# A depthwise convolution moved from per-lag steps to one triangular product per channel, in a fused conditional residual block

## The reference, cut to what matters

```python
x = x + depthwise_causal_conv(x, w=cond)            # x: (B=32, T=32, C=256) f32, cond: (K=32, C=256)
ada = cond @ ada_w + ada_b                          # six chunks: shift, scale, gate, twice
h = ln(x) * (1 + scale1) + shift1                   # layer norm over C, one (shift, scale) per batch
q, k, v = split(h @ qkv_w + qkv_b)                  # 16 heads of 128
a = softmax(q k^T / sqrt(128)) v                    # within a batch: 32 x 32 scores
y = x + gate1 * (a @ out_w + out_b)
g = gelu((ln(y) * (1 + scale2) + shift2) @ ffn_w1 + ffn_b1)
out = x + y + gate2 * (g @ ffn_w2 + ffn_b2)
```

## Time and profile before

| | |
|---|---|
| median of 3 runs | 336.91 us (336.74 to 336.94) |
| profiled execution, first to last instruction | 337.2 us |
| PE busy | 319.7 us, 95% |
| PE weight loads | 269.0 us, 80% |
| DVE busy | 180.0 us, 53% |
| ACT, POOL busy | 152.7 us, 80.8 us |

### The profile page before, as it was taken

The page is one execution under the profiler, slowest core; times in us unless marked ns, Lnnn a source line. Parts: engine busy times, 40 slices in busy tenths (PEclk is TensorE's granted clock), DMA queues, the critical chain, the costliest instruction groups (busy, mean ns, idle before and its releaser), DMA issues.

```text
span 337.2 us, 6425 instructions
## 1 busy us (share of the span) xinstructions
PE 319.7 (95%) x2655; PEld 269.0 (80%) x2655; DVE 180.0 (53%) x354; ACT 152.7 (45%) x269; POOL 80.8 (24%) x78
## 2 busy tenths in 40 slices
PE   5969599999999999999999999999999999899994
PEld 4959496868888888888888888888898778588884
DVE  4959979866606224333441532631625699783232
ACT  6421032423366525526625535653443557742910
POOL 5606510031034103006303003500201444430400
PEclk9959789999999999999999999999999999999998
DMA  7822100010004202002300101210200000000011
GB/s 247 318 68 62 62 3 0 2 65 0 0 2 126 64 0 64 0 2 68 122 0 0 62 0 41 86 63 0 64 2 0 3 2 0 0 2 0 0 64 62
DMA packets 9607, 14.56 MB, mean 43 GB/s; under 512 B 520, under 2 KB 5744, under 8 KB 9584
## 3 DMA queue, kind: packets, MB, share of 16 engines
q1 hardware_dynamic: 9536, 14.19, 12.9%
q10 hardware_dynamic: 48, 0.03, 0.0%
HBM read 13.18 MB, written 1.05 MB: 42 GB/s over the span
## 4 chain that ended last, share of the span: by engine, by line
PE 79%; DVE 17%; issue 1%; DMA 1%; ACT 1%; DVEq 0%
PE bank L930 16%; PE bank L931 16%; PE bank L932 16%; PE bank L1006 7%; DVE xc L537 6%; PE bank L939 4%; PE bank L941 4%; PE bank L940 4%; PE bank L863 3%; PE bank L992 3%; PE bank L853 3%; DVE pt L642 2%; DVE yacc L747 1%; DVE xc L547 1%; DMA crow<-in_cond_dram 1%
## 5 line engine op out<-in xcount | busy, mean ns | idle before, releaser
L278 POOL TENSOR_TENSOR wl<-raw,wh 128x512 fp32r<-128x512 f32 x40 | 53.1, 1349 | 181.2 <-ACT wh L333 181.2
L930 PE MATMUL bank<-x1h,wl 128*128 128x512 f32 (+1 forms) x176 | 67.8, 385 | 0.0
L931 PE MATMUL bank<-x1l,wh 128*128 128x512 f32 (+1 forms) x176 | 65.9, 374 | 0.0
L932 PE MATMUL bank<-x1h,wh 128*128 128x512 f32 (+1 forms) x176 | 65.8, 374 | 0.0
L394 ACT ACTIVATE pool<-bank,bg 128x512 f32<-128x512 f32 x56 | 38.6, 688 | 57.3 <-PE bank L932 57.0
L653 DVE SCALAR_TENSOR_TENSOR ol<-bank,bT,oh 128x512 fp32r<-128x512 f32 x32 | 23.9, 749 | 46.8 <-ACT oh L423 46.0
L537 DVE SCALAR_TENSOR_TENSOR xc<-x,condT,xc 128x240 f32<-128x240 f32 (+32 forms) x114 | 39.4, 417 | 0.0
L930 PEld LDWEIGHTS bank<-x1h,wl 128*128 128x128 f32 x176 | 34.0, 193 | 6.3 <-issue 0.7
L931 PEld LDWEIGHTS bank<-x1l,wh 128*128 128x128 f32 x176 | 34.0, 193 | 5.8 <-issue 0.2
L932 PEld LDWEIGHTS bank<-x1h,wh 128*128 128x128 f32 x176 | 33.9, 193 | 5.7
L1006 PEld LDWEIGHTS bank<-pt,pool 128*128 128x128 f32 x256 | 31.9, 191 | 3.4 <-issue 0.9
(11 more groups left out here) (105 smaller groups left out, 450.8 us busy)
## 6 DMA issues: line engine op xcount, KB each, us to landing
raw<-in_L_cond_qkv_w_dram SPq DMA_DIRECT2D x12, 512.0 KB, 3.8
raw<-in_L_cond_out_w_dram SPq DMA_DIRECT2D x4, 512.0 KB, 3.4
raw<-in_L_cond_ffn_w_dram SPq DMA_DIRECT2D x4, 512.0 KB, 3.4
adaw<-in_L_cond_ada_w_dram SPq DMA_DIRECT2D x1, 1024.0 KB, 11.3
out_dram<-pool SPq DMA_DIRECT2D x4, 256.0 KB, 2.2
pool<-in_x_dram SPq DMA_DIRECT2D x2, 256.0 KB, 3.1
adaw<-in_L_cond_ada_w_dram SPq DMA_DIRECT2D x1, 512.0 KB, 5.3
pool<-in_x_dram SPq DMA_DIRECT2D x1, 512.0 KB, 6.1
```

Of the source, the lines that this page charges most:

```text
L278: g.tensor_tensor(wl[:, cols], raw[:, cols], wh[:, cols].bitcast(F32), ALU.subtract)\
L930: pe.matmul(dst, wl[:, w_cols], a_hi, start=start, stop=False)
L931: pe.matmul(dst, wh[:, w_cols], a_lo, start=False, stop=False)
L932: return pe.matmul(dst, wh[:, w_cols], a_hi, start=False, stop=stop)
```

## The change

The lags, the diagonals and `x0`'s part in the convolution go. In their place:

1. x is loaded in two pieces of 512 KB. It is spread from (batch in tile, time) x channel to `xq`, whose partitions are 4 channel groups of 64 x 32 time steps. That is 16 copies of 32 partitions x 512 elements, 5 on ACT and 11 on DVE. Source runs stride over 256 elements.
2. `cond` is written to a new DRAM tensor `cond_padded` with 31 rows of zeros behind it: two DMAs on ACT's queue, one DRAM to DRAM (32 rows), one from an SBUF tile of zeros (31 rows). SP waits for both, then reads `toep` back in four DMAs of 256 KB, each to 32 partitions, with overlapping source rows. `toep[:, j, :, c]` is then the 32x32 triangular matrix of channel slot c of group j, in 128 rows of which the others are zeros. The zeros are four memsets of 128x2048, two on DVE, two on POOL.
3. `conv(k)`, k = 0 to 3: 64 products each, stationary `toep[:, j, :, c]` (128x32, elements 256 bytes apart), moving `xq[:, c]` (128x32), into partition group j of bank `CB[k]`. 256 products do the whole convolution for all tokens.
4. Four copies of 128x512 take it to `conv_out` (ACT 0 and 2, DVE 1 and 3).
5. `turn(n)`, n = 0 to 3: 32 products each, stationary `conv_out[:, 32 slots, batch]` (elements 128 bytes apart), moving `pick` (128x64, zeros and ones), bring it to channels on partitions. They accumulate on x's transposes, which were put into the same banks `XB[n]` with no end of group, so that the residual sum needs no other instruction. Four copies take the banks to `xc`.
6. Order: all of this stands ahead of the norms. `modulation(1)` and `(2)` become one, ahead of `project_chunk(0)`. `mean(2)`, `var(2)`, `spread(2)` stand among the chunk projections, and the first attention joins the regular `unit(0, 1, first=True)`. The biases' DMAs move from SP's queue to ACT's; ada_w stands ahead of the first group's weights. POOL's clearing of `pt` waits for the turns, because `conv_out` lies in its memory.

```diff
-    PE_LAGS = [[0] + list(range(6, 17)), [0] + list(range(3, 18)), [0] + list(range(8, 15))]
-    DVE_LAGS = [[j for j in range(1, T) if j not in lags] for lags in PE_LAGS]
+        XB, CB = PB + YB[0:1], [S_BANK, OB[0], OB[1], YB[1]]
+        cond_pad = nc.dram_tensor("cond_padded", [QB, 2 * T - 1, SLOTS], F32)
+        def pad_rows(r0, r1):
+            return bass.AP(cond_pad, r0 * SLOTS, [[SLOTS, r1 - r0], [(2 * T - 1) * SLOTS, QB], [1, SLOTS]])
+        SPREAD_BY_ACT = [(i, g) for g in range(QB) for i in range(QB)][1::3]
...
@@ sync
-            load_x(0)
-            load_x(1)
+            for n in range(HALVES):
+                sp.dma_start(xtok[:, 4 * n:4 * n + 4, :], x_v[:, 4 * n:4 * n + 4, :]).then_inc(s_x[n], 16)
+            sp.wait_ge(s_pad, 32)
+            for g in (0, 2, 1, 3):
+                sp.wait_ge(s_tz[g // 2], g % 2 + 1)
+                sp.dma_start(toep[T * g:T * (g + 1), g, :, :].rearrange("p u s -> p (u s)"),
+                             bass.AP(cond_pad, g * (2 * T - 1) * SLOTS, [[SLOTS, T], [1, T * SLOTS]]))\
+                    .then_inc(s_toep, 16)
             load_adaw(0, 0, ADA1 * P)
-            load_x(2)
...
+            load_adaw(1, ADA1 * P, ADA * P)
             load_group(0)
-            load_adaw(1, ADA1 * P, ADA * P)
...
@@ gpsimd
-            for n in range(1, ND, 2):
...
+            for q in (2, 3):
+                g.memset(toep[:, q, :, :], 0.0).then_inc(s_tz[1], 1)
...
@@ scalar
             a.dma_start(crow[:, :], cond).then_inc(s_row[0], 16)
+            a.dma_start(pad_rows(0, T), cond.rearrange("k (g s) -> k g s", g=QB)).then_inc(s_pad, 16)
+            a.wait_ge(s_zr, 1)
+            a.dma_start(pad_rows(T, 2 * T - 1), zrows[:, :].rearrange("k (g s) -> k g s", g=QB)).then_inc(s_pad, 16)
+            for at, src in ((B_QKV, qkv_b), (B_ADA, ada_b), (B_OUT, out_b), (B_F1, ffn_b1), (B_F2, ffn_b2)):
...
+            for i, g in SPREAD_BY_ACT:
+                a.activation(xq[T * g:T * (g + 1), :, i, :],
+                             xtok[T * i:T * (i + 1), :, SLOTS * g:SLOTS * (g + 1)].rearrange("p n s -> p s n"),
+                             ACT.Copy).then_inc(s_xq[0], 1)
...
@@ vector
-            conv(0, 0, len(DVE_LAGS[0]))
-            conv_sum(0)
+            for g in range(QB):
+                for i in range(QB):
+                    if (i, g) not in SPREAD_BY_ACT:
+                        v.tensor_copy(xq[T * g:T * (g + 1), :, i, :],
+                                      xtok[T * i:T * (i + 1), :, SLOTS * g:SLOTS * (g + 1)]
+                                      .rearrange("p n s -> p s n")).then_inc(s_xq[1], 1)
+            conv_copy(1)
+            conv_copy(3)
+            xc_copy(1)
             centre(0)
...
@@ tensor
+            def conv(k):
+                if k == 2:
+                    pe.wait_ge(s_btc, 1)
+                if k == 3:
+                    pe.wait_ge(s_cond, 1)
+                for s in range(CBLK):
+                    c = CBLK * k + s
+                    for j in range(QB):
+                        m = pe.matmul(CB[k][T * j:T * (j + 1), B * s:B * (s + 1)], toep[:, j, :, c],
+                                      xq[:, c, :, :].rearrange("p i n -> p n i"), start=True, stop=True)
+                m.then_inc(s_cv, 1)
+            def turn(n):
+                if n == 0:
+                    pe.wait_ge(s_co[0], 2)
+                    pe.wait_ge(s_co[1], 2)
+                    pe.wait_ge(s_const, 4)
+                tiles = XB[n][:, :].rearrange("p (k b t) -> p k b t", k=CT, b=XB_B)
+                for b in range(XB_B):
+                    for q in range(QB):
+                        s0 = T * (q % 2)
+                        m = pe.matmul(tiles[T * q:T * (q + 1), :, b, :], conv_out[:, s0:s0 + T, XB_B * n + b],
+                                      pick[:, q // 2, :, :], start=False, stop=(b == XB_B - 1), skip_group_check=True)
+                m.then_inc(s_sel, 1)
+            pe.wait_ge(s_toep, 16 * QB)
+            pe.wait_ge(s_xq[0], len(SPREAD_BY_ACT))
+            pe.wait_ge(s_xq[1], QB * QB - len(SPREAD_BY_ACT))
+            for k in range(NX):
+                conv(k)
...
+            turn(0)
+            turn(1)
+            mean(0)
             pe.wait_ge(s_adaw[0], 16)
             modulation(0)
-            mean(0)
-            conv(1, 0, 2)
             var(0)
-            conv(1, 2, 4)
+            turn(2)
+            mean(1)
             spread(0)
-            conv(1, 4, len(PE_LAGS[1]))
+            turn(3)
+            var(1)
+            pe.wait_ge(s_adaw[1], 16)
+            pe.wait_ge(s_adat, ADA_STEPS[0])
+            modulation(1)
...
             pe.wait_ge(s_lo, CT)
             pe.wait_ge(s_adat, 2)
-            project_chunk(0, (0,))
-            mean(1)
...
-            conv(2, 0, 4)
+            project_chunk(0, (0, 1))
+            spread(1)
+            project_chunk(0, (2, 3))
+            mean(2)
+            project_chunk(0, (4, 5))
             pe.wait_ge(s_lo, CT * 2)
-            project_chunk(1, range(0, 5))
+            project_chunk(1, (0,))
+            var(2)
+            project_chunk(1, (1, 2))
+            spread(2)
+            project_chunk(1, (3, 4))
             scores(0, 0)
             project_chunk(1, (5,))
-            conv(2, 4, len(PE_LAGS[2]))
...
-            modulation(1)
...
-            project(0, 1, range(0, 9))
-            scores(0, 1)
-            project(0, 1, (9, 10, 11))
+            pe.wait_ge(s_lo, CT * 3)
+            pe.wait_ge(s_adat, ADA_STEPS[1])
+            unit(0, 1, first=True)
             with pe.Fori(1, NG - 1) as hg:
```

More of the change, by code:

```diff
@@ L84, in cond_resid_block_kernel @@
         pool = sb("pool", [P, 16 * PIECE])
+        with nc.sbuf_tensor("conv_out", [P, SLOTS, B], F32) as conv_out:
+            pass
         pt = sb("pt", [P, HALVES, GH, TG, P])
+        with nc.sbuf_tensor("adaw", [P, CT, ada_w.shape[1]], F32) as adaw:
+            pass
         oh = sb("oh", [P, GH, HT], F32R)
@@ L91, in cond_resid_block_kernel @@
         ident = sb("ident", [P, P])
+        pick = sb("pick", [P, 2, CT, T])
+        zrows = sb("zrows", [T - 1, C])
         ones = sb("ones", [P, P])
@@ L105, in cond_resid_block_kernel @@
         vt = sb("vt", [P, TG, T])
-        with nc.sbuf_tensor("diag", [P, ND, P], F32) as diag, \
-                nc.sbuf_tensor("adaw", [P, CT, ada_w.shape[1]], F32) as adaw:
+        with nc.sbuf_tensor("toep", [P, QB, T, SLOTS], F32) as toep:
             pass
@@ L513, in _ @@
         def _(v):
+            v.memset(zrows[:, :], 0.0).then_inc(s_zr, 1)
+            for q in (0, 1):
+                v.memset(toep[:, q, :, :], 0.0).then_inc(s_tz[0], 1)
             v.wait_ge(s_condt, 1)
-            v.tensor_copy(condT[:, :, :], S_BANK[:, 0:CT * B].rearrange("p (k b) -> p k b", k=CT))\
+            v.tensor_copy(condT[:, :, :], CB[3][:, 0:CT * B].rearrange("p (k b) -> p k b", k=CT))\
                 .then_inc(s_cond, 1)
-            v.wait_ge(s_xt, 1)
-            for ct in range(CT):
-                v.tensor_copy(part(x0, ct, CHUNKS[0]), OB[0][:, 256 * ct:256 * (ct + 1)]).then_inc(s_xe[0], 1)
@@ L713, in _ @@
             softmax_transpose(0, 0)
-            conv_sum(2)
-            centre(2)
-            o_low(0, 0, (0, 1))
-            scale_up(2)
-            var_eps(2)
-            o_low(0, 0, (2,))
-            norm(2)
-            shift(2)
-            o_low(0, 0, (3,))
-            x1_low(2)
-            modulation(1)
-            modulation(2)
-            add_y(0, 0, first=True)
-            one_plus(2, SCALE2)
-            softmax_front(0, 1)
-            softmax_back(0, 1)
+            unit(0, 1, first_y=True)
             unit(1, 0, first_y=True)
@@ L842, in conv @@
-            def conv(n, i0, i1):
-                nt, last = CHUNKS[n][1], len(PE_LAGS[n]) - 1
-                for i in range(i0, i1):
-                    j = PE_LAGS[n][i]
-                    for ct in range(CT):
-                        d = DIAG_LAGS.index(j)
-                        pe.wait_ge(s_diag[ct], d + 1)
-                        xs = by_batch(part(x0, ct, CHUNKS[n]))
-                        dst = by_batch(CONV_BANKS[n][ct][:, 0:nt])
-                        m = pe.matmul(dst[:, :, j:], diag[:, CT * d + ct, :], xs[:, :, :T - j],
-                                      start=(i == 0), stop=(i == last))
-                        if i == last:
-                            m.then_inc(s_cpe, 1)
@@ L858, in mean @@
-            def mean(n):
-                pe.wait_ge(s_const, 2)
-                pe.wait_ge(s_in, CT * (n + 1))
+            for n in range(NX):
+                pe.wait_ge(s_x[n // 2], 16)
+                for i in range(2 * CT):
+                    ct, t = divmod(i, 2)
+                    pe.matmul(XB[n][:, P * i:P * (i + 1)], xtok[:, 2 * n + t, ct * P:(ct + 1) * P], ident[:, :],
+                              start=(i == 0), stop=False, is_transpose=True, skip_group_check=True)
+            pe.wait_ge(s_row[1], 16 * 5)
```

255 lines of the change are left out of this document (110 added, 145 removed).

## The result

The changed kernel takes 334.14 us (median of 20 executions, 332.06 to 337.12), the kernel before 337.99 us beside it (20 executions, 336.74 to 339.52). The ratio is 0.9887, with a 95% interval of 0.986 to 0.9914 (it leaves out the one of the 20 executions that is more than 1.5% above its kernel's fastest, 337.12 us). So the change makes the kernel 1.1% faster, 3.9 us where 19.2 were forecast.

A forecast was written before the change was run, and what follows sets the result against it. PE's instruction list was taken as the bound, except where DVE's lags held it. First projection 3.2 us later, at 37.5, and units 19.2 us earlier gave a span of 318.0, median 317.7 us; range 312.3 to 325.5.

The forecast's parts named there:

- the convolution starts: Start of PE's convolution products: expected at 13.7 us, once x has landed and been spread.
- the convolution: PE's 256 small products: 7.7 us, at the scores' pace with the first 5 us at half clock.
- the handover: Between convolution and turns: the last `conv_copy`, 0.69 us, and a handover of 0.15 us.
- from the turns to the first projection: PE's list of turns, means, variances, modulations and spread before the first projection: 15.3 us without a wait.
- the regular units and the end: Everything from the first regular unit onward: no instruction's work altered, only reached 19.2 us earlier.
- rival 2: Convolution and turns: strided operands halve the small products' pace, +5.2 us each, total 328 us; chance 0.12.
- the clock that I had put at half for 5 us: Convolution: after about 7 us idle, PE runs 123 products at half clock for 5 us.
- Rival 4: Convolution and turns: four partition groups stop overlapping, 41 ns per product, +31 us, total 349 us; chance 0.05.
- rival 1: Convolution start: zero rows' write lands at about 13, convolution 4.2 us late, 322 us; or clock wakes late, 323; chance 0.20.
- My cover of 3.6 us for `toep`: Before the convolution: `toep` loads landed by 10 us, hidden behind x's spreading with 3.6 us to spare.
- Stretch two: First projection to the regular units: 72.4 us before, 22.4 us leave it, becoming 50.0 us.
- From span to time: Whole kernel: the median time was taken to lie 0.3 us below the span, 318.0 to 317.7 us.

The follow-up runs named there:

- e1: Changed kernel with the convolution's stationary operand reading neighbouring elements of toep (output not the reference's): 331.1 us, one execution.
- e3: Changed kernel with both operands of the convolution read in the order of memory (output not the reference's): 332.67 us, ratio 0.9816.
- e9: Changed kernel with the convolution as a loop of 8 passes over 32 products, strides kept (output not the reference's): 334.9 us, one execution.
- e8: Changed kernel with the convolution as a loop of 8 passes over 32 products, operands neighbouring (output not the reference's): 328.0 us, one execution.
- e7: Changed kernel with both convolution operands in memory order, plus two 512-column products before each of blocks 1, 2 and 3: 331.71 us, one execution.
- e10: Changed kernel with only the turns' stationary operand reading neighbouring elements (output not the reference's): 333.89 us, one execution.
- e11: Changed kernel unchanged, repeated for a comparison on one chip: 333.04 us, six executions, ratio 0.9873.
- e5: Changed kernel with convolution operands exchanged, 64 products instead of 256, 128 neighbouring moving columns (output not the reference's): 326.1 us, one execution.
- e2: Changed kernel with only the convolution's moving operand read in the order of memory (output not the reference's): 335.7 us, one execution.
- e6: Changed kernel with convolution operands exchanged, 64 products instead of 256, moving columns 256 bytes apart (output not the reference's): 325.3 us, one execution.

## Why the prediction was wrong

In spans, forecast 318.0 and measured 333.6:

| step | forecast | measured | off |
|---|---|---|---|
| the convolution starts | 13.7 | 14.7 | +1.0 |
| the convolution | 7.7 | 17.2 | +9.5 |
| the handover | 0.8 | 0.85 | +0.1 |
| from the turns to the first projection | 15.3 | 15.9 | +0.6 |
| from there to the regular units | 50.0 | 50.8 | +0.8 |
| the regular units and the end | 230.5 | 234.1 | +3.6 |

**The step that failed** is the convolution: "256 products of exactly the form of the scores, 64 in 1.30 us". The form is the same in shape only. It gave 7.7 us where 17.2 were measured, and this term is 9.5 of the 15.6 us by which the span was off. Three things were wrong in it.

- *Stride.* The scores' stationary elements are neighbours, these are 256 bytes apart. e1 and e3 against the changed kernel, and e9 against e8 (29.4 against 15.6 ns per record), show it. This was rival 2, with its mechanism right, and a chance of 0.12 too small: my argument against it looked at the moving operand, which costs 2 ns, while the stationary one is it. Twice the time was priced, and about twice is what the stride costs (1.9 times between e8 and e9); that the convolution ran at three times the scores' pace comes from the third point. The Trainium skill ("SBUF — State Buffer", the section on the DMA port swizzle) said that a step into a new line of 16 bytes costs. The trace agrees for steps of 256 bytes; the moving operand's steps of 32 bytes, each into a new line too, cost only 1 to 2 ns per record.
- *Supply.* The scores are one run of 128 records; the convolution is 512 with nothing long between them. Behind the first 203, the instructions of 128 records arrive per 3.5 to 4.0 us, 27 to 31 ns per record. This stood in no rival, nor could the rows of before show it, which have no such run. The sum put the supply at nothing. e3, e7 and e8 show it, and the packets of 16 KB. By e3, it alone would have made 15.7 us.
- *What even a loop with neighbours takes*, 15.6 ns per record at full clock instead of 10.2: 8.0 us. Its last two passes go at 10.2 with pauses of 0.2 us, the six before take 1.04 us each; what slows those stays open. That this nearly equals the forecast 7.7 is chance; the clock that I had put at half for 5 us was at half for 3.3, and cost nothing, since 30 ns were needed at either level. Rival 4, groups that stop overlapping at 41 ns a record, wasn't met: 30 was the pace, and one operand's stride alone halved it. The result lies above the range of every rival but rival 4, because no rival had two of these costs at once.

**The start** was 1.0 us late by the pad, rival 1's mechanism at a quarter of its price: the write of 31 rows landed at 7.98, not at 13. My cover of 3.6 us for `toep` was eaten by this (3.2 us against the forecast 4.8) and by the loads, of which the last took 5.4 us instead of 3.1. That this DMA also blocks the queue that stands ahead of ACT's copies I had not seen. DVE's copies were faster than taken (6.8 instead of 7.9 us), and were not what PE waited for.

**The list to the first projection**: the turns took 6.5 us instead of 5.2 (their stride, e10), the rest 0.7 less than summed. No norm step and no weight was late there, as argued. **Stretch two** was right within 0.8 us, and that although the clock stood at 0.50 from 49 to 52 us, which at half pace costs some 1.5 us.

**The regular units** I had taken as unchanged. In a run like e11 they are: from the scores at 119.99 to the end 329.0 are 209.0 us. The same scores of the kernel before, in its timeline:

```profile
128.07 1.11 PE L992 MATMUL bank<-pool 128*32 128x32 f32 x108
```

Before: 337.2 less 128.07, 209.1. In the changed kernel's profiled execution: 333.6 less 120.92, 212.7. So the 3.6 us are the stall at 122 and the half clock behind it (0.58 mean from 124 to 128), which come and go between executions. The stall is the same supply of instructions: it falls behind a fixed record of a run of short products, and in all four profiles that have it PE goes on 2.2 to 2.4 us behind a late packet of 16 KB. No run took it away alone. Why it is there in some executions, and what else spreads the times over 5 us, stays open.

**From span to time** I took 0.3 us off; the profiled executions whose own time is known lie 1.8 us above their spans (335.38 and 333.6). The kernel before has the same 1.8 us in its timed executions (338.56 and 336.8), so it changes no difference; its profiled execution with a span of 337.2 then took about 339.0 us (an estimate).

The gain in stretch two (21.6 us, forecast 22.4) was thus real; but the way to the first projection grew by 14.5 us (34.27 to 48.72) where 3.2 were forecast, and 3.6 went into the regular units: 21.6 less 18.1 is what is left in the profile.

## What to carry to other kernels

Price a product by its operands' strides, not by its shape alone, above all the stationary one's. Count the instructions of a run of short products: beyond the first two hundred records, PE got 128 per 3.5 to 4 us here, so a rewrite that trades long products for many short ones can be bound by their number. Fewer and wider products (e5) or a loop (e8) avoid the limit, and other work of PE between the products (e7) costs nothing. When removing a suspected cause gains almost nothing, look whether idle time took its place before dropping it: two limits of the same size hide one another.

## What the runs showed of the hardware

- Copies out of PSUM were slowed while PE read operands 256 bytes apart. ACT's 128x512 copies (L364) take 2.34 us on average in the changed kernel and 0.60 in e1, e3, e5 and e7, where only steps of 32 bytes or none are left. In e2, whose stationary operand alone is strided, ACT's take 1.66. DVE's copy (L557) during the convolution takes 1.85 us in the changed kernel and 0.69 in e1 and e3. It cost nothing here: PE waits only for DVE's last copy, which runs with PE idle, in 0.69.
- TensorE's granted clock fell to 0.50 at 48.9 us, though PE had no idle time since 32.8; it was up again at 52.3. In e10 it fell earlier (mean 0.67 from 38.66 on), in e6 not at all between 37 and 52 us. What makes it fall there stays open.
- A strided copy of 32x512 within SBUF takes 0.59 us on DVE and 1.06 on ACT.
- Instructions come in packets of 16 KB, 256 to a packet, which is 64 bytes for one (an estimate from e5's and the changed kernel's counts). In a run of short products PE went on 2.2 to 2.4 us behind a packet's transfer, and the packets of e3 came 3.45 us apart (26.90 and 30.35) with the DMA engines otherwise at rest.
